# Row-tiled products of 64 rows for the softmax maxima of a decoder layer, one maximum over two PSUM banks, and TensorE's attention units written out

## The reference, cut to what matters

```python
qn = _rmsnorm(q, q_gamma) * dh ** (-0.5)      # 8 heads of 64 numbers
kn = _rmsnorm(k, k_gamma)
sim = jnp.einsum('bhid,bhjd->bhij', qn, kn)   # 2048 x 2048 for each head
attn = jax.nn.softmax(sim, axis=-1)
out = jnp.einsum('bhij,bhjd->bhid', attn, v)
```

## Time and profile before

| | |
|---|---|
| median of three executions | 2375.18 us (2373.36 to 2376.58) |
| the profiled execution, its own time | 2378.47 us |
| its span, first to last instruction | 2376.8 us |
| busy: TensorE (PE) | 2208.2 us, 93% |
| busy: TensorE weight loads (PEld) | 1263.1 us, 53% |
| busy: VectorE (DVE) | 1565.7 us, 66% |
| busy: ScalarE (ACT) | 1610.6 us, 68% |
| busy: GpSimd (POOL) | 1485.4 us, 62% |
| mean granted TensorE clock | 0.967 |

### The profile page before, as it was taken

The page is one execution under the profiler, slowest core; times in us unless marked ns, Lnnn a source line. Parts: engine busy times, 40 slices in busy tenths (PEclk is TensorE's granted clock), DMA queues, the critical chain, the costliest instruction groups (busy, mean ns, idle before and its releaser), DMA issues. The chain is left out here.

```text
span 2376.8 us, 65765 instructions
## 1 busy us (share of the span) xinstructions
PE 2208.2 (93%) x22384; PEld 1263.1 (53%) x22384; DVE 1565.7 (66%) x2599; ACT 1610.6 (68%) x1828; POOL 1485.4 (62%) x978
## 2 busy tenths in 40 slices
PE   6987999999997999899969879999999978998999
PEld 3543666666665455444435436666666654554444
DVE  6986777777776766743269867777777767667532
ACT  3554999999997566621045549999999985566210
POOL 3325898989898586721033258989898975866210
PEclk9997999999999999999979979999999999999999
DMA  4320000000002301100043200000000023011000
GB/s 102 62 37 4 2 9 9 9 9 9 9 0 50 81 2 46 37 19 18 36 107 58 39 2 2 9 9 9 9 9 9 0 52 79 1 46 37 19 18 35
DMA packets 103504, 65.17 MB, mean 27 GB/s; under 512 B 76498, under 2 KB 76498, under 8 KB 103378
## 3 DMA queue, kind: packets, MB, share of 16 engines
q1 hardware_dynamic: 103378, 63.57, 12.8%
HBM read 46.69 MB, written 8.39 MB: 23 GB/s over the span
## 5 line engine op out<-in xcount | busy, mean ns | idle before, releaser
L693 POOL TENSOR_TENSOR probs_l<-probs,probs_h 128x1024 f16<-128x1024 f32 x448 | 988.7, 2233 | 166.0 <-PE bank L745 127.9
L814 DVE TENSOR_REDUCE pm<-bank 128x1 f32<-128x512 f32 x1024 | 680.5, 688 | 276.5 <-PE bank L701 272.0
L797 ACT ACTIVATE probs_h<-bank,shift 128x1024 f16<-128x1024 f32 x512 | 567.6, 1109 | 52.1 <-PE bank L717 52.1
L805 ACT ACTIVATE probs<-bank,shift 128x1024 f32<-128x1024 f32 x512 | 570.2, 1114 | 38.9 <-DVE probs_l L828 30.6
L716 PE MATMUL bank<-q_hh,ko 128*128 (+1 forms) x1024 | 392.1, 383 | 32.8 <-DMA q_lm<-nm 17.1
L701 PE MATMUL bank<-ko,q_hh 128*128 (+1 forms) x1024 | 397.4, 391 | 20.6 <-PEq L331 12.1
L717 PE MATMUL bank<-q_lm,k_h 65*128 (+1 forms) x1024 | 392.6, 383 | 0.0
L730 PEld LDWEIGHTS bank<-v_hl,probs_h 128*128 128x128 f16 x4096 | 288.3, 98 | 65.6 <-issue 8.1
L730 PE MATMUL bank<-v_hl,probs_h 128*128 (+1 forms) x4096 | 321.3, 193 | 0.2
L732 PE MATMUL bank<-v_hl,probs_h 128*128 (+1 forms) x4096 | 319.0, 194 | 0.0
L732 PEld LDWEIGHTS bank<-v_hl,probs_h 128*128 128x128 f16 x4096 | 268.2, 96 | 59.2 <-issue 0.6
(11 more groups left out here) (215 smaller groups left out, 4203.8 us busy)
## 6 DMA issues: line engine op xcount, KB each, us to landing
xt_a<-in_x SPq DMA_DIRECT2D x32, 256.0 KB, 2.7
q_lm<-in_x SPq DMA_DIRECT2D x32, 256.0 KB, 3.1
ko<-in_L_ffn_W SPq DMA_DIRECT2D x32, 256.0 KB, 3.9
q_hh<-q_hh SPq DMA_DIRECT2D x32, 128.0 KB, 2.5
ko<-k_h SPq DMA_DIRECT2D x32, 128.0 KB, 2.7
q_lm<-nm SPq DMA_DIRECT2D x256, 0.2 KB, 4.9
out<-bo_b SPq DMA_DIRECT2D x16, 256.0 KB, 2.0
out<-xbo_b SPq DMA_DIRECT2D x16, 256.0 KB, 2.0
```

What stands on the lines that cost most here:

```text
L693: pool.tensor_tensor(probs_l[:, p % 2, :], probs[:, p % 2, :], probs_h[:, p % 4, :], ALU.subtract).then_inc(pl_pool, 1)
L797: act.activation(probs_h[:, p % 4, :], SB[p % 2][:, :], ACT.Exp, bias=shift[:, 0:1]).then_inc(ph_ready, 1)
L805: act.activation(probs[:, p % 2, :], SB[p % 2][:, :], ACT.Exp, bias=shift[:, 0:1]).then_inc(p_ready, 1)
L814: dve.tensor_reduce(pm[:, s, k:k + 1], MB[k % 2], AX_X, ALU.max).then_inc(mx_free, 1)
```

## The change

The maxima leave out the low part of k. `k_hl` is turned over: the low part lies in partitions 0 to 63, the high part in 64 to 127. A product for maxima then takes 64 rows, q high times k high. Two of them, for two chunks of 512 keys of the same 128 queries, are issued one behind the other, the first at rows 0 to 63 (`tile_position=(0, 0)`, from `k_h1`), the second at rows 64 to 127 (`(64, 0)`, from `k_hl`), into the two banks of one pair. VectorE reduces both banks in one operation of 1024 columns. There are 8 such pairs of products and 8 reductions in a unit, with one pair of banks for all of them (`mx_free` starts with one credit; before, two). Both products of a step stand before `values_high`. VectorE's `output` now comes after the third of 8 reductions, `probs_low` after the sixth. TensorE's loop over units 2 to 29 is replaced by 28 units written out.

```diff
-                            sp.dma_start(k_hl[0:DH, :, tok], k_h1[0:DH, :, tok]).then_inc(a_dup, 16)
+                            sp.dma_start(k_hl[DH:P, :, tok], k_h1[0:DH, :, tok]).then_inc(a_dup, 16)
...
-                    MB = banks[4:6]
+                    MB = pairs[2]
...
-                        def unit_max(r, k):
-                            pe.wait_ge(mx_free, (U0 + r) * 16 + k + 1)
-                            pe.matmul(MB[k % 2], qf[:, bass.ds(r * CT + k // 4 * P, P)],
-                                      k1[:, bass.ds(r // CH * N + k % 4 * CT, CT)], start=True, stop=True)\
-                                .then_inc(mx_ready, 1)
+                        def unit_max(r, j):
+                            pe.wait_ge(mx_free, (U0 + r) * 8 + j + 1)
+                            pe.nop(nofuse=True)
+                            qcols = bass.ds(r * CT + j // 2 * P, P)
+                            for part, keys in enumerate((k2, k1)):
+                                rows = slice(DH * part, DH * part + DH)
+                                kcols = bass.ds(r // CH * N + (j % 2 * 2 + part) * CT, CT)
+                                pe.matmul(MB[:, part * CT:(part + 1) * CT], qf[rows, qcols], keys[rows, kcols],
+                                          start=True, stop=True, tile_position=(DH * part, 0)).then_inc(mx_ready, 1)
...
-                                        for k in range(2):
-                                            unit_max(1 + p // 4, p % 4 * 4 + half * 2 + k)
-                                    elif maxed:
-                                        unit_max(u + LA, 2 * p + half)
+                                        unit_max(1 + p // 4, p % 4 * 2 + half)
+                                    elif maxed and half == 0:
+                                        unit_max(u + LA, p)
...
-                        with pe.Fori(1, UNITS // 2 - 1) as i:
-                            for s in range(2):
-                                unit(i * 2 + s, s)
+                        for u in range(2, MAXED):
+                            unit(u, u % 2)
...
-                            dve.wait_ge(mx_ready, (U0 + r) * 16 + k + 1)
-                            dve.tensor_reduce(pm[:, s, k:k + 1], MB[k % 2], AX_X, ALU.max).then_inc(mx_free, 1)
+                            dve.wait_ge(mx_ready, ((U0 + r) * 8 + j + 1) * 2)
+                            dve.tensor_reduce(pm[:, s, j:j + 1], MB[:, :], AX_X, ALU.max).then_inc(mx_free, 1)
...
-                            for k in range(16):
+                            for j in range(8):
                                 if maxed:
-                                    reduce_max(u + LA, k, s)
-                                if k == 4 and not first:
+                                    reduce_max(u + LA, j, s)
+                                if j == 2 and not first:
                                     output(u - 1, 1 - s)
-                                if k == (6 if first else 2 * (DVE_PAIR + 1)):
+                                if j == (3 if first else DVE_PAIR + 1):
                                     probs_low(u)
```

More of the change, by code:

```diff
@@ L297, in _ @@
                                    pattern=[[-1, P]], channel_multiplier=1).then_inc(s_pool, 1)
-                for s, credits in ((a_y, 2), (a_v_ready, 1), (a_ssq, 1), (a_rinv, 1), (a_qk, 2), (a_ht_free, 2), (lo_done, 2), (mx_free, 2),
+                for s, credits in ((a_y, 2), (a_v_ready, 1), (a_ssq, 1), (a_rinv, 1), (a_qk, 2), (a_ht_free, 2), (lo_done, 2), (mx_free, 1),
                                    (pl_pool, PAIRS - 1), (m_ready, 2 * ROW), (nm_ready, 2), (o_free, 2),
@@ L558, in heads_low @@
                             tok = bass.ds(t * P, P)
-                            for which, (high, low, row, g) in enumerate(((q_hh, q_lm, 0, qg), (k_h1, k_hl, DH, kg))):
+                            for which, (high, low, g) in enumerate(((q_hh, q_lm, qg), (k_h1, k_hl, kg))):
                                 for odd in range(2):
@@ L563, in heads_low @@
                                     low_part = dve.scalar_tensor_tensor(
-                                        out=low[row:row + DH, odd::2, tok], in0=src,
+                                        out=low[0:DH, odd::2, tok], in0=src,
                                         scalar=g[DH * odd:DH * odd + DH, :], in1=high[0:DH, odd::2, tok],
@@ L624, in decoder_layer @@
                     probs_l = sb(ph, "probs_l", [P, 2, 2 * CT], F16)
-                    pm = sb(ph, "pm", [P, 2, 16], F32)
+                    pm = sb(ph, "pm", [P, 2, 8], F32)
                     nm = sb(ph, "nm", [P, 2, TPC], F16)
@@ L772, in unit @@
                                         values_low(u - 1, PAIRS - 2 + p, OB[1 - s])
-                        for k in range(16):
-                            unit_max(0, k)
+                        for j in range(8):
+                            unit_max(0, j)
                         pe.wait_ge(a_ones, 2 * b + 2)
@@ L808, in _, with reduce_max @@
                     def _(dve):
-                        def reduce_max(r, k, s):
-                            if k == 0:
+                        def reduce_max(r, j, s):
+                            if j == 0:
                                 dve.wait_ge(nm_ready, U0 + r + 1)
-                            dve.wait_ge(mx_ready, (U0 + r) * 16 + k + 1)
-                            dve.tensor_reduce(pm[:, s, k:k + 1], MB[k % 2], AX_X, ALU.max).then_inc(mx_free, 1)
+                            dve.wait_ge(mx_ready, ((U0 + r) * 8 + j + 1) * 2)
+                            dve.tensor_reduce(pm[:, s, j:j + 1], MB[:, :], AX_X, ALU.max).then_inc(mx_free, 1)
                         def negate_max(r, s):
-                            dve.wait_ge(mx_free, (U0 + r) * 16 + 18)
+                            dve.wait_ge(mx_free, (U0 + r) * 8 + 9)
                             dve.wait_ge(m_ready, ROW * (U0 + r + 1))
-                            dve.tensor_reduce(nm[:, s, :], pm[:, s, :].rearrange("p (a k) -> p a k", k=4), AX_X, ALU.max,
+                            dve.tensor_reduce(nm[:, s, :], pm[:, s, :].rearrange("p (a k) -> p a k", k=2), AX_X, ALU.max,
                                               negate=True).then_inc(nm_ready, 1)
@@ L856, in unit @@
                             if first:
-                                for k in range(16):
-                                    reduce_max(1, k, 1)
+                                for j in range(8):
+                                    reduce_max(1, j, 1)
                                 negate_max(1, 1)
-                            for k in range(16):
+                            for j in range(8):
                                 if maxed:
-                                    reduce_max(u + LA, k, s)
-                                if k == 4 and not first:
+                                    reduce_max(u + LA, j, s)
+                                if j == 2 and not first:
                                     output(u - 1, 1 - s)
-                                if k == (6 if first else 2 * (DVE_PAIR + 1)):
+                                if j == (3 if first else DVE_PAIR + 1):
                                     probs_low(u)
@@ L868, in unit @@
                                 negate_max(u + LA, s)
-                        for k in range(16):
-                            reduce_max(0, k, 0)
+                        for j in range(8):
+                            reduce_max(0, j, 0)
                         negate_max(0, 0)
```

## The result

The changed kernel takes 2594.5 us (median of 4, 2593.71 to 2596.61) against 2375.06 us (4 runs): a ratio of 1.0926, 95% interval 1.0907 to 1.0944. The forecast was 2389 us with a range of 2373 to 2414. Slower was right; the size was not: +219 us for a forecast of +14. The profiled execution has a span of 2592.1 us and a mean granted clock of 0.928.

A forecast was written before the change was run, and what follows sets the result against it. A cycle through TensorE, VectorE's `probs_low` and ScalarE was taken to bound the kernel. Per batch row, +3.6 (start), +2.0 (unit 0), +0.8 (27 units) and +0.6 (body's end) made 7.0, +14 for two: 2389 us, range 2373 to 2414.

The forecast's parts named there:

- `probs_low` to exponential 1.25: Link of the body's cycle: ScalarE's exponential starts 1.25 us after VectorE starts `probs_low`.
- the sum for the unit after: Period of a body unit after the change: a 5.04 us chain plus six steps, 12.15, makes 17.19 us against 17.16.
- The last rival: GpSimd sets the pace: its step 5 subtraction overlaps `probs_low` wholly, adding up to 0.3 us; no chance given.
- a period above 17.5 us: Sign in the next profile that the forecast unit period, 17.1 to 17.3 us, was wrong, through the switches.
- the switches: TensorE getting into and out of tiled products around each pair: 0.10 us each way, 0.20 a step.
- the start: Start of the phase, before the first scores: one pair of banks makes eight turns of 1.92 us, +3.6 us per batch row.
- unit 0: First unit, two pairs in a step: two turns of 1.72 us make 3.43 against 3.10, about +2.0 us per batch row.
- The loop's gap: End of TensorE's loop body: 0.58 us lost once in two units, 0.29 a unit, given back by writing out.
- the dearer switch: Rival: switches in TensorE's steps cost 0.30 us, the unit takes 17.79 us, the kernel 2423 us; chance 0.16.
- the free one: Rival: switches cost nothing or nearly, a step takes 1.82 to 1.9 us, the kernel 2381 us; chance 0.12.
- late instructions: Rival: instructions come late in the written-out units, so the loop's 0.29 us stay; +16, 2405 us; chance 0.06.
- the cheap reduction: Rival: VectorE's 1024-column reduction takes less than 1.22 us; at 0.95 us the kernel takes about 2363 us; chance 0.10.

The follow-up runs named there:

- e4: The changed kernel with the four scores products of step 7 issued three times over (same data, same banks, released once); 2505.3 us.
- e5: The kernel before with TensorE's loop over units 2 to 29 written out, all else as before; 2357.2 us.
- e8: The changed kernel with GpSimd's subtraction of step 5 over 512 columns instead of 1024; 2477.1 us.

## Why the prediction was wrong, step by step

**The step that failed** is "`probs_low` to exponential 1.25" in the sum for the unit after. It took the 1.22 us of the earlier trace rows for a property of the instruction. It was that of coming first. The measured size is 753.68 - 750.66 = 3.02 us from `probs_low` to exponential. The numbers for the comparison were in the prediction's reach: the sum itself puts `probs_low` at 0.44 + 1.14 = 1.58 us after the product, which is already behind GpSimd's 1.48. And GpSimd, which waits for `values_low` of step 3, had to come still nearer to the product, as no second product stands ahead of that work any more (it came at 1.38): I never wrote down its new time. The rows said that order matters: the earlier trace rows shows GpSimd stretched from 2.1 to 2.75 us beside `probs_low`. The last rival took it as a matter of GpSimd alone, at up to 0.3 us, and left it inside the range; it names no effect on VectorE. The Trainium skill, "SBUF — State Buffer", "SBUF: two separate sides", states the rule: a VectorE instruction with two SBUF inputs and a GpSimd instruction that reads SBUF contend for a port pair that they share under an exclusive lock, and whichever starts first keeps it for its whole instruction while the other is fully blocked. The trace agrees, with the 1.09 us between the two ends at both widths of GpSimd's operation and at starts 0.22 and 1.21 us apart.

The prediction's own sign of being wrong, a period above 17.5 us, was right as a sign, but it named the switches as the cause.

**The second failure** is that in the body no term and no rival held TensorE's clock. The wait alone would have given 27 x 2 x 1.72 = 93 us; e4 shows another 89 us for the half clock that follows. With the start and unit 0, below, 27 us, these make 209 of the 219. No run takes the rest apart. In the profiled executions the end of the phase, from unit 28 on, takes 6 us more in each batch row, where the sum had 0.6, and the later phases, whose code is the same, 4.5 us less.

**Unit 0** was priced +2.0 us and took +10.2 in the first batch row and +8.1 in the second (step 1 of unit 0 to step 1 of unit 1: 25.0 us before, 35.3 and 33.1 after). The turn is 1.81 us and not 1.72 at full clock. Two turns make a step of 3.63, 0.5 over before and not 0.33. The first four steps take 4.4 to 4.8 us (clock 0.50 from 210 to 220 us), where before only the first two were slow, 4.1 and 4.0. The rest is `probs_low` behind GpSimd once more, 2.51 us long, and low clock after it. How much of it is clock alone stays open. **The start** was priced +3.6 and took +4.4: a turn of 2.02 us, not 1.92, since the product came 0.15 us after the reduction's end and not 0.06.

**What held.** The switches: starts in one step of the changed kernel are

```profile
400.02 0.38 PE L721 MATMUL bank<-q_lm,k_h 65*128 65x512 f16 x1
400.34 0.39 PE L706 MATMUL bank<-k_h,q_hh 64*128 64x512 f16 x1
400.34 0.39 PE L706 MATMUL bank<-ko,q_hh 64*128 64x512 f16 x1
400.66 0.20 PE L734 MATMUL bank<-v_hl,probs_h 128*128 128x65 f16 x1
```

0.32 and 0.32 for 0.22 each: 0.10 to get in, 0.10 to get out, both products at once. The step of 2.025 came out at 2.03. The wide reduction took 1.22 us. The loop's gap was real: e5 measured 18 us for it, against 16. The body was blocked by no wait for `mx_free`, on a cover of 0.04 us. One product in the rivals is off, without effect here: 27 x 0.6 x 2 is 32 us and not the 34 of the dearer switch. Neither the dearer switch nor the free one, neither late instructions nor the cheap reduction took place; the cause was a case that had no chance of its own.

## What to carry to other kernels

Where two engines may block one another, write down for both at what time each starts, before and after an edit, and what it costs when the order turns; a lead of 0.45 us of `probs_low` over GpSimd was all that kept this loss away. A latency in a trace can depend on who came first: look for the rare long records of the same instruction (here 1996 ns beside a median of 1215 in the kernel before, four times in 64). An instruction that another engine waits for can sometimes move to where nobody contends: here that alone was worth 1.2% of the kernel before, and 1.8% with the units written out.

## What the runs showed of the hardware

- A subtraction of 1024 columns on VectorE with both inputs in SBUF takes 1.22 us when it starts before GpSimd's, and ends 1.09 us after GpSimd's end when it starts 0.22 us after it (2.99 us long) or 1.21 us after it (1.99 us long). GpSimd's goes from 2.13 to 2.75 us when it starts 0.45 us after VectorE's.
- TensorE, idle for 1.62 and, 0.4 us of work later, for 0.73 us, went to 1.2 GHz for some 3.5 us (755.30 to 758.8) in each unit of the body; the mean granted clock of that stretch is 0.51. With one idle time of 0.73 us left in that place (e4) it stayed at 2.4 GHz; with 0.65 and 0.73 us (e8) it fell in 6 of 27 units.
- Two products of 64 rows at different rows of the array start within 0.01 us of each other, into two banks. A pair between products of full height costs 0.42 us (400.66 - 400.02 - 0.22), one product of full height 0.22.
